# Where the log counts are added: clamp and add on VectorE, one tile in four by transfer, and edge rows joined in the first stage

## The reference, cut to what matters

```
h = (x @ W).reshape(N, 4, 24)
e = leaky_relu(alpha_s[src] + alpha_d[dst], 0.2)
m = segment_max(e, dst);  ex = exp(e - m[dst]);  den = segment_sum(ex, dst)
out = segment_sum(h[src] * (ex / den[dst]), dst) + b          # x = relu(out), 3 times
...
msg = relu(x[src] + edge_attr @ We + be)                      # last layer
aggr = segment_sum(msg, dst)
```

## Time and profile before

| | us |
|---|---|
| median of three timed executions | 5863.4 |
| the profiled execution's own time | 5863.81 |
| its span, first to last instruction | 5862.1 |
| PE, DVE, ACT, POOL busy | 3511.6, 3123.5, 2625.6, 3883.7 |
| L330, 806 count additions (POOL) | 1253.9 busy, 385.4 idle before them |
| main part of the first attention layer, 1970 to 2590: PE, DVE, ACT, POOL busy | 570.42, 342.37, 549.26, 476.54 |

### The profile page before, as it was taken

How to read it: one execution, slowest core, us unless ns; L and a number is a source line. 1 busy time by engine, 2 the same in 40 slices (tenths; PEclk the granted TensorE clock), 3 DMA queues, 4 the chain that set the end, 5 groups by cost and what they waited for, 6 DMA issues and landing times. The chain is left out here.

```text
span 5862.1 us, 68109 instructions
## 1 busy us (share of the span) xinstructions
PE 3511.6 (60%) x25247; PEld 2219.0 (38%) x25248; DVE 3123.5 (53%) x3383; ACT 2625.6 (45%) x4143; POOL 3883.7 (66%) x3309
## 2 busy tenths in 40 slices
PE   3211222221034699988999889997868781667764
PEld 2211111111034455555555555554433330455542
DVE  3644555554369555445555455555579992333323
ACT  1000000000023689888888789894059891222211
POOL 1888888888884577666776578773020787777772
PEclk7555555555566899999999999998989995677765
DMA  8222222222279699757997479875542332332222
GB/s 296 20 18 20 20 18 10 1 1 0 9 251 361 169 195 199 161 115 150 195 193 156 103 164 201 184 153 152 178 166 79 109 130 74 110 81 74 75 53 24
DMA packets 427191, 683.75 MB, mean 117 GB/s; under 512 B 177678, under 2 KB 272397, under 8 KB 422768
## 3 DMA queue, kind: packets, MB, share of 16 engines
q0 software_dynamic: 236096, 287.22, 31.9%
q1 hardware_dynamic: 172432, 350.48, 17.8%
q10 hardware_dynamic: 18336, 41.70, 2.1%
HBM read 540.73 MB, written 138.43 MB: 116 GB/s over the span
## 5 line engine op out<-in xcount | busy, mean ns | idle before, releaser
L330 POOL DMA_INDIRECT counts<-plcell_add,plcell_slot x806 | 1253.9, 1556 | 385.4 <-issue 223.2
L1704 POOL DMA_INDIRECT emxg<-xtab,emsrc x856 | 944.0, 1103 | 448.4 <-issue 257.8
L714 ACT ACT_TABLE_LOAD x1 | 1.3, 1283 | 1613.2 <-PE mtps L702 1613.2
L377 PE MATMUL plpsR<-plpiece,plbefore 128*128 128x500 bf16 (+1 forms) x81 | 47.1, 582 | 813.8 <-DVE plranked L507 800.6
L422 DVE TENSOR_REDUCE plnlow<-plsame 128x13 f32<-128x1664 bf16 x62 | 117.0, 1888 | 661.6 <-DMA counts<-plcell_add,plcell_slot 661.5
L1788 PE MATMUL dotbanks<-emmsg,emsame 128*128 128x96 f32 x1712 | 316.3, 344 | 237.4 <-DVE emsame L1968 230.1
L1176 ACT ACTIVATE ga1prob<-ga1psE,ga1src_fifth 128x512 f32<-128x512 f32 (+1 forms) x700 | 407.2, 680 | 81.8 <-PE ga1psE L1281 79.1
L1176 ACT ACTIVATE ga2prob<-ga2psE,ga2src_fifth 128x512 f32<-128x512 f32 (+1 forms) x700 | 407.5, 683 | 77.0 <-PE ga2psE L1281 74.1
L1176 ACT ACTIVATE ga0prob<-ga0psE,ga0src_fifth 128x512 f32<-128x512 f32 (+1 forms) x700 | 407.1, 678 | 77.7 <-PE ga0psE L1281 74.7
L1788 PEld LDWEIGHTS dotbanks<-emmsg,emsame 128*128 128x128 f32 x1712 | 287.2, 250 | 382.2 <-issue 379.5
L1281 PE MATMUL ga0psE<-ident,ga0logit 128*128 128x128 f32 x2500 | 394.5, 288 | 55.8 <-DMA ga0logit<-log_counts 32.7
(11 more groups left out here) (403 smaller groups left out, 8577.9 us busy)
## 6 DMA issues: line engine op xcount, KB each, us to landing
ga0logit<-log_counts POOLq DMA_DIRECT2D x88, 512.0 KB
ga1logit<-log_counts POOLq DMA_DIRECT2D x88, 512.0 KB
ga2logit<-log_counts POOLq DMA_DIRECT2D x88, 512.0 KB
counts<-plzeros SPq DMA_DIRECT2D x32, 1250.0 KB, 32.7
mthalf<-counts SPq DMA_DIRECT2D x50, 800.0 KB
log_counts<-mtlogs SPq DMA_DIRECT2D x25, 1600.0 KB
ginhalf<-counts SPq DMA_DIRECT2D x50, 800.0 KB
dotlogs<-log_counts ACTq DMA_DIRECT2D x25, 1600.0 KB
```

The costliest lines, as they stand in the source:

```text
L330: nc.gpsimd.indirect_dma_start(counts[w][:, :], bass.IndirectOffsetOnAxis(ap=cell_slot[:, g % 2, j:j + 1], axis=0), cell_add[:, g % 2, j:j ...
L377: nc.tensor.matmul(psR[:, f // RANK_BANK, 0:k * BINS], before[:], piece[:, n % 2, f:f + k, :].rearrange("p t b -> p (t b)"), start=True, s ...
L714: nc.scalar.activation(logs[:, n % OUTS, q, :], ps[:, u % 3, 0:BW], ACT.Ln, bias=tiny[:, 0:1], scale=math.e).then_inc(log_made, 1)
L1704: nc.gpsimd.indirect_dma_start(xg[:, h, t, :], None, xtab[:, :], bass.IndirectOffsetOnAxis(ap=src[:, g, t:t + 1], axis=0)).then_inc(gather ...
```

## The change

Four edits are made.

1. In `gat_attend`, `ADDED` shrinks to tile 3 alone. For the other tiles VectorE clamps in the same way (`clamp_kept`) and then adds the loaded log counts with a `tensor_tensor` (`finish_logit`). ScalarE's `add_bias` is gone. All tiles of a run are clamped first, and then the kept ones are added. `output(j - 1)` stands behind the whole of run 4's logits and no longer between two of its tiles. The mask loads wait for `logit_ready`.
2. In `begin`, SP loads the features of 62 groups into `whole` (rows of 32 out of 34 numbers), ScalarE copies the ends into them, and SP stores joined rows to DRAM (`edge_rows`), one group for every two additions in table 1.
3. `edge_scatter` loads slots once and joined rows once per group; its copies, the clearing and two of its loads are gone, and it has three stages.
4. The spare cells' zeros are written first, as one contiguous row of 256 bytes for each table.

```diff
-                    sp.dma_start(part[NP * NP:NP * NP + P, :], zeros[:, 0:1]).then_inc(done, 16)
+                for part, done in zip(counts, zeroed):
+                    sp.dma_start(part[NP * NP:NP * NP + P, :].rearrange("(p f) o -> p (f o)", p=1), zeros[0:1, 0:P]).then_inc(done, 16)
...
+                for g in range(NG):
+                    sp.wait_ge(added[1], 16 * (4 * SORTED_GROUPS + 2 * g + 1))
+                    if g + 1 < NG:
+                        load_whole(g + 1)
+                    sp.wait_ge(whole_made, g + 1)
+                    sp.dma_start(edges["rows"][:, g * G:(g + 1) * G, :], whole[:, g % WHOLE_BUFS, :, :]).then_inc(whole_stored[g % WHOLE_BUFS], 16)
...
+            pool.dma_start(stage[:, k, :, :], edges["rows"][:, g * G:(g + 1) * G, :]).then_inc(rows_loaded[k], 16)
-            nc.gpsimd.tensor_copy(stage[:, k, :, 0:ED], feat[:, k, :, :]).then_inc(staged, 1)
-            nc.gpsimd.tensor_copy(stage[:, k, :, ED:RW], ends[:, m, :, :]).then_inc(staged, 1)
...
-        ADDED = (2, 3)
-        BIAS_AT = (1, 5)
+        ADDED = (3,)
+        MASK_FREE_AT = (3, 4, 6)
...
+                def clamp_kept(r, q):
...
+                    nc.vector.tensor_scalar(logit[:, r % L_BUFS, q, 0:width], src_row[:, h, first:first + width], dst_bias[:, j % 2, q, h:h + 1],
+                                            low_bias[:, j % 2, q, h:h + 1], ALU.add, ALU.max).then_inc(kept_clamped, 1)
...
+                    dve.wait_ge(kept_clamped, kept_count[r] + kept_tiles(j).index(q) + 1)
+                    dve.wait_ge(mask_loaded[k], 16 * (uses + 1))
                     part = logit[:, r % L_BUFS, q, 0:width]
-                    nc.vector.scalar_tensor_tensor(part, src_row[:, h, first:first + width], least[:, block_first[j] + q, h:h + 1], part, ALU.max, ALU.add).then_inc(logit_ready, 1)
+                    nc.vector.tensor_tensor(part, part, mask[:, k, 0:width], ALU.add).then_inc(logit_ready, 1)
...
-                    for i in range(MOST + 1):
-                        if ahead is not None and i < len(kept_tiles(ahead)):
-                            finish_logit(r + AHEAD, kept_tiles(ahead)[i])
-                        if run == 2 and j and i == 1:
-                            output(j - 1)
+                        for q in kept_tiles(ahead):
+                            clamp_kept(r + AHEAD, q)
+                        for q in kept_tiles(ahead):
+                            finish_logit(r + AHEAD, q)
+                    if run == 2 and j:
+                        output(j - 1)
...
-                    nc.scalar.activation(logit[:, r % L_BUFS, q, 0:width], mask[:, k, 0:width], ACT.Identity, bias=dst_bias[:, j % 2, q, h:h + 1]).then_inc(act_biased, 1)
```

More of the change, by code:

```diff
@@ L58 @@
 HI_BITS = 9
+WHOLE_BUFS = 3
 ZF = 5000
@@ L333, in _ @@
                     pool.wait_ge(added[w], 16 * adds_before(ET, w))
+            @block.scalar
+            def _(act):
+                act.wait_ge(ends_made, 1)
+                for g in range(NG):
+                    k = g % WHOLE_BUFS
+                    uses = range(k, g + 1, WHOLE_BUFS)
+                    act.wait_ge(whole_loaded[k], sum(32 if n * G < EREST else 16 for n in uses))
+                    nc.scalar.activation(whole[:, k, :, ED:RW], ends[:, g * G:(g + 1) * G, :], ACT.Copy).then_inc(whole_made, 1)
             @block.tensor
@@ L767, in source_rows, with edge_scatter @@
     return row_kept, len(chunks)
[L770 to L776, removed]
+def edge_scatter(nc, ctx, edges, tag, first, last):
+    STAGES = 3
     count = last - first
[L778 to L786, removed]
-    def steps(pool):
[L789 to L794, removed]
+    slot = ctx.enter_context(nc.sbuf_tensor(tag + "slot", [P, max(count, 1) * G], i32))
+    stage = ctx.enter_context(nc.sbuf_tensor(tag + "stage", [P, STAGES, G, RW], f32))
+    slots_loaded = nc.alloc_semaphore(tag + "slots_loaded")
+    rows_loaded = [nc.alloc_semaphore(f"{tag}rows_loaded{k}") for k in range(STAGES)]
+    scattered = [nc.alloc_semaphore(f"{tag}scattered{k}") for k in range(STAGES)]
+    def steps(pool):
@@ L796, in load @@
         def load(i):
[L798 to L801, removed]
+            k, g = i % STAGES, first + i
             if i >= STAGES:
-                pool.wait_ge(staged, 2 * (i - STAGES + 1))
@@ L804, in load @@
-            pool.dma_start(rows[0:P - 1, :], most[:, g * G * ED:(g + 1) * G * ED]).then_inc(feat_loaded[k], 16)
-            n = min(G, EREST - g * G)
-            if n > 0:
-                pool.dma_start(rows[P - 1:P, 0:n * ED], rest[:, g * G * ED:(g * G + n) * ED]).then_inc(feat_loaded[k], 16)
+                pool.wait_ge(scattered[k], 16 * G * (i // STAGES))
+            pool.dma_start(stage[:, k, :, :], edges["rows"][:, g * G:(g + 1) * G, :]).then_inc(rows_loaded[k], 16)
+        pool.dma_start(slot[:], edges["slot"][:, first * G:last * G]).then_inc(slots_loaded, 16)
@@ L809, in steps @@
         load(0)
+        pool.wait_ge(slots_loaded, 16)
         for i in range(count):
-            k, m = i % STAGES, i % LISTS
+            k = i % STAGES
             if i + 1 < count:
                 load(i + 1)
-            pool.wait_ge(feat_loaded[k], sum(loads(n) for n in range(k, i + 1, STAGES)))
-            pool.wait_ge(list_loaded[m], 32 * (i // LISTS + 1))
-            if i >= STAGES:
-                pool.wait_ge(scattered[k], 16 * G * (i // STAGES))
-            nc.gpsimd.tensor_copy(stage[:, k, :, 0:ED], feat[:, k, :, :]).then_inc(staged, 1)
@@ L968, in _ @@
                         _, j, c, q, free = load
-                        wait(sp, act_biased, free)
+                        wait(sp, logit_ready, free)
                         k, _ = mask_slot(j * RUNS + c * HEADS, q)
@@ L1096, in _ @@
                     for q in kept_tiles(0):
+                        clamp_kept(r, q)
+                    for q in kept_tiles(0):
                         finish_logit(r, q)
```

71 lines of the change are left out of this document (40 added, 31 removed).

## The result

The kernel after takes 6215.7 us (median of five, 6203.23 to 6217.63), the kernel before 5864.6 in the same series. The ratio is 1.0589, with an interval of [1.0569, 1.0609]. I had forecast 5686 us and given "slower" 0.11.

A forecast was written before the change was run, and what follows sets the result against it. It took ScalarE to lead in the attention layers and POOL's additions in the first stage, with VectorE deciding after the change. 5863.8 - 25 (first stage) - 153 (three layers) = 5686 us; range 5615 to 5800.

The forecast's parts named there:

- SP loads 62 times some 1650 pieces of 128 bytes... I take nothing for it; the end above is a landing at 4.6: First stage, joined rows: 0.7 us of delay per addition is free, so the feature loads were priced at nothing.
- an upper end of 56: First stage: feature loads making additions land at 4.6 us, 0.9 us for each of 62, 56 us at most.
- rival 3: First stage: row loads delay the additions by 56 us, total 5742; chance 0.16 together with one case of rival 1.
- additions are short, and the wait ends with the instruction that is running: Attention layers: argument against POOL's scatters being held long by VectorE, made against rival 1.
- d = 1.95: Mean scatter in us if VectorE's clamps shut POOL out: 622 us a layer for POOL, total 5767.
- rival 1: Attention layers: POOL becomes the bound as scatters meet busy VectorE, up to 6028; slower case 0.11, d = 1.95 within 0.16.
- POOL loses copies and loads and is not the bound: `make_tables` and the layers: the lighter scatter on POOL was costed at nothing.
- I cost it at nothing, TensorE's lag hides it; without that cover it is 1 us a run, 48 a layer: Attention layers: the run's one accumulating transfer, issued behind its clamp, lands about when the additions end.
- the attention arithmetic on VectorE: Attention layers: VectorE's clamps and additions set blocks of about 74 to 76 and 89 us, layer 595 against 646.2.
- the coupling through `output`: Four-tile blocks: TensorE stands 5 us at run 3 for the output, VectorE then waits about 4, making 89.
- the spare cells: First stage: zeros written first and as one row bring the seventh addition some 25 us sooner.
- masks in time: Attention layers: mask loads land nearly in time, 0.5 us a chunk, 10 a layer; ends 0 and 64.

The follow-up runs named there:

- e5: The kernel after with each feature load cut at partition 112 into two transfers, 128-byte pieces kept: 5835.4 us, ratio 0.9944 to the kernel before.
- e7: e5 with each kept tile clamped and added to at once, so no two additions stand next to each other: 5724.2 us, ratio 0.9759.
- e4: The kernel after with the attention of before (spare cells, joined rows and lighter scatter kept): 6167.8 us, ratio 1.0530.
- e8: e5 without the edge rows' scatters in the three attention layers: 5869.9 us, ratio 1.0009; only the layers' times can be read.
- e9: e7 with the output of the block before worked out ahead of run 4's logits: 5671.6 us, ratio 0.9662.
- e6: e4 with the feature loads cut at partition 112 as in e5: 5794.4 us, ratio 0.9882.
- e2: The kernel before with only the spare cells' zeros written first and as one row: 5831.0 us, ratio 0.9943.
- e10: e7 with features loaded as packed rows of 1664 bytes, cut at partition 112 and spread by ScalarE: 5749.7 us, ratio 0.9796.
- e1: The kernel after with features loaded packed, 127 uncut pieces of 1664 bytes, spread by ScalarE: 6107.3 us, ratio 1.0423.

## Why the prediction was wrong

1. **Failed: "SP loads 62 times some 1650 pieces of 128 bytes... I take nothing for it; the end above is a landing at 4.6".** The step priced only what the loads would do to the additions' landing, and from a row of a time in which nothing else was loaded. It also charged one late addition for each load, 62 in all, where 420 additions waited for landings, 432.5 us together. And it never asked how long one load takes itself. It takes 16.8 us, 62 of them come one behind the other, and so SP's chain became the stage's end (2010). e5 gives the size by difference: 384 us of the stage (2023.9 to 1639.8), against an upper end of 56. Of these, 238 are the delayed additions, which rival 3 had in the right place and far too small, and 146 the chain that runs on behind them, which no rival had. This step alone turns the sign.
2. **Failed: "additions are short, and the wait ends with the instruction that is running".** For most scatters that begin during the first addition, and for half of those that begin right ahead of it, it ends with the last instruction of the row. The row used had a single addition of 3.48 us running, so it could not show a row of several. The order "all clamps, then all additions" made rows of 3.5 and 3.9 us. e7 showed it. The value d = 1.95, reached in rival 1, was nearly measured (1.94, 1.86, 1.85), and so were its 622 us for POOL (626.9 in the blocks and more in the tail), but by another way, so this match is luck. The Trainium skill, "SBUF — State Buffer", Who interferes with whom, says that `tensor_scalar` in a two-port mode shuts GpSimd out. No scatter here waited for the clamps like that (1.27 us at 2412.07, beside three of them, and 1.53 at most); whether the clamps ran in such a mode no trace shows. The same section says that an instruction with two SBUF inputs contends with a GpSimd one that reads SBUF; that agrees with e7, where a scatter outlasts the running addition by 0.9 us. What the traces show beyond it is that a row of three without a pause counts as one for 104 of the 120 scatters that begin in its first addition.
3. **Failed: "POOL loses copies and loads and is not the bound".** It was so close to it that the lighter scatter alone is worth 61 us in three layers (e4), and with slow scatters POOL was nearly full and ended the layer. A busy share of 477 in 620 did not tell it: some 70 us of issue gaps belong to the engine's own pace.
4. **Failed: "I cost it at nothing, TensorE's lag hides it; without that cover it is 1 us a run, 48 a layer".** This is the run's one accumulating transfer. It had no cover: it stood behind long scatters in POOL's queue, and TensorE waited 39 to 43 us a layer for it. That is the path on which the traces show slow scatters lengthening a block, and it is more than the 32 us that the first layer's blocks lie above the forecast (626.9 against 595).
5. **Held in the main: the attention arithmetic on VectorE.** Three-tile blocks of the first layer within 1.2 us, additions at 1.21 and 1.35 (1.24 and 1.37 forecast), and near 89 for four tiles once the scatters are gone (87 to 95 in e8) or the couplings loosened (86 to 92 in e9). The forecast gain of 153 us in the layers was not reached by this edit alone: with two changes of order e9 gains 172, but the lighter scatter is in it, and against e6, which has that scatter and the attention of before, it is 114.
6. **Held: the coupling through `output`.** 44 us in e9's layers, 3.7 for each of the twelve four-tile blocks if all of it is put on them.
7. **Held: the spare cells**, 25 forecast and the seventh addition 23.2 us sooner, 34 in the median (e2). **Held: masks in time.** VectorE never waited for them, so the 10 us a layer that I had added were not there either.

Two terms of the working are slightly off, without effect: by its own terms block 0 is 69.7 + 4.2 = 73.9 and not 73.6, and the clamps are some 43 % of a run and not 41 %.

With the measured sizes put in, the sum has no large term missing: 5863.8 - 25 + 384 - 16 = 6207, against 6215.7.

## What to carry to other kernels

For a load that a change adds, work out first how long one takes on its own and how many follow each other; cut it so that its partition count divides well (112 and 15 instead of 127). When one engine's transfers wait for another engine's instructions, the order of these counts as much as their number: alternate the kinds (111 us here), and keep a queue's urgent transfer from standing behind one that can be held. Count an engine's issue gaps with its busy time (521 and 69 of 640 us here), and ask who waits for what it issues late.

## What the runs showed of the hardware

- One direct transfer over 127 partitions moved 206 KB in 16.8 us and held the queue's next issue for all that time; cut into 112 and 15 partitions it went in 1.5 us.
- GpSimd's indirect transfers waited for VectorE's additions of two tensors (5.1 us in the first case shown). Of those that began in the first of three additions in a row, 104 of 120 ended behind the third; of those that began in the second, 53 of 61 ended behind the second. Beside clamps alone they took 1.12 us on average, against 0.97 beside an idle VectorE.
- TensorE idled for 7.3 us up to 2411.4. Its granted clock was 1.00 from 2400 to 2404, 0.50 from 2408 to 2420, 0.61 in the next 4 us and 1.00 from 2424.
- Packed pieces of 1664 bytes slowed the two-byte additions more than 128-byte ones did: 19 us in 806 with the cut (e10), and 2.7 to 3.1 us apart instead of 2.4 to 2.6 without it (e1). Why stays open.
